# Second attention: the stores of its relative terms in halves of 64 rows, narrower by the columns that nothing reads

## The reference

```python
x = L0_attn_a_hidden_states
x = x + _L0_attn_a_ref(_layernorm(x, axis=-1),  ...)
x = x + _L0_ffn_ref(_layernorm(x, axis=-1),  ...)
x = x + _L0_attn_b_ref(_layernorm(x, axis=-1),  ...)
x = x + _L0_ffn_ref(_layernorm(x, axis=-1),  ...)
```

```python
def heads(x):
    return x.reshape(B, S, H, D).transpose(0, 2, 1, 3)
q = heads(hidden_states @ Wq + bq)
k = heads(hidden_states @ Wk + bk)
v = heads(hidden_states @ Wv + bv)
scores = jnp.einsum('bhqd,bhkd->bhqk', q, k)
pos_l = jnp.arange(S)[:, None]
pos_r = jnp.arange(S)[None, :]
dist_idx = pos_l - pos_r + M - 1
pos_emb = dist_emb[dist_idx]
rel_q = jnp.einsum('bhld,lrd->bhlr', q, pos_emb)
rel_k = jnp.einsum('bhrd,lrd->bhlr', k, pos_emb)
scores = (scores + rel_q + rel_k) / jnp.sqrt(jnp.asarray(D, scores.dtype))
probs = jax.nn.softmax(scores, axis=-1)
ctx = jnp.einsum('bhqk,bhkd->bhqd', probs, v)
ctx = ctx.transpose(0, 2, 1, 3).reshape(B, S, E)
```

## Time and profile before

| | us |
|---|---|
| median of 3 runs (4907.82 to 4912.31) | 4911.35 |
| the profiled execution | 4912.15 |
| its span | 4910.4 |
| stage b1 | 2244 to 3058 |
| stage b2 | 3058 to about 3950 |

### The profile page before, as it was taken

The page is one execution under the profiler, slowest core; times in us unless marked ns, Lnnn a source line. Parts: engine busy times, 40 slices in busy tenths (PEclk is TensorE's granted clock), DMA queues, the critical chain, the costliest instruction groups (busy, mean ns, idle before and its releaser), DMA issues.

```text
span 4910.4 us, 102424 instructions
## 1 busy us (share of the span) xinstructions
PE 3915.1 (80%) x31924; PEld 2380.9 (48%) x31924; DVE 2889.9 (59%) x6305; ACT 2635.3 (54%) x6550; POOL 1689.6 (34%) x1383
## 2 busy tenths in 40 slices
PE   2999999999488888734666565999999945888886
PEld 1555555554255555522222222677777723555554
DVE  2555555555577777543444443566666665777775
ACT  1555555554367777523333333566666624777774
POOL 0000000000588888523222222111111116878774
PEclk9999999999799999965555555999999977999998
DMA  3222222221111111027999999777777711111111
GB/s 118 87 78 78 78 78 80 81 78 53 49 25 23 27 27 23 17 71 293 380 381 385 380 381 369 269 262 260 248 272 250 256 43 52 25 26 25 25 23 32
DMA packets 374686, 701.06 MB, mean 143 GB/s; under 512 B 54180, under 2 KB 161016, under 8 KB 374568
## 3 DMA queue, kind: packets, MB, share of 16 engines
q1 hardware_dynamic: 330536, 565.25, 33.6%
q0 software_dynamic: 44032, 134.30, 7.4%
HBM read 336.53 MB, written 314.64 MB: 133 GB/s over the span
## 4 chain that ended last, share of the span: by engine, by line
PE 51%; DMA 13%; DVE 10%; issue 9%; POOL 7%; ACT 4%; SPq 2%; DVEq 1%; POOLq 0%; ACTq 0%
DMA rel_k<-b_stage_k 12%; PE ps L332 5%; PE ps L1465 5%; PE ps L340 5%; PE ps L351 5%; PE ps L1474 5%; PE ps L1456 3%; PE ps L1485 3%; DVE f_rs L1028 2%; POOL f_rn L758 2%; PE ps L866 2%; DVE f_rc L1025 2%; POOL f_rot L756 2%; PE ps L1357 2%; DVE b_stage_k L1381 2%
## 5 line engine op out<-in xcount | busy, mean ns | idle before, releaser
L1381 DVE COPY b_stage_k<-ps 128x640 f32<-128x640 f32 (+2 forms) x512 | 359.1, 722 | 469.6 <-DMA rel_k<-b_stage_k 410.3
L430 ACT ACTIVATE a_p<-a_s,a_min 128x512 f32<-128x512 f32 x512 | 366.0, 715 | 470.3 <-DVE a_min L474 470.3
L1378 ACT ACTIVATE b_stage_q<-ps 128x640 f32<-128x640 f32 (+2 forms) x512 | 316.0, 624 | 505.4 <-PE ps L1360 388.0
L474 DVE CUSTOM_DVE_ANT_0 a_s<-ps,a_table 128x512 f32<-128x512 f32 x512 | 333.5, 689 | 374.5 <-PE ps L332 371.9
L1539 ACT ACTIVATE c_p<-c_s,c_min 128x512 f32<-128x512 f32 x512 | 370.2, 723 | 290.7 <-PE ps L1474 180.3
L1357 PE MATMUL ps<-b_e,b_st_k 48*128 48x512 bf16 (+1 forms) x512 | 305.9, 597 | 261.1 <-DVE b_stage_k L1381 261.1
L1574 DVE CUSTOM_DVE_ANT_0 c_s<-ps,c_rq 128x512 f32<-128x512 f32 x512 | 352.8, 689 | 200.8 <-PE ps L1465 188.1
L188 POOL COPY y<-ln_rows 128x512 f32 x32 | 19.9, 621 | 1304.8 <-DVE ln_rows L180 1304.8
L949 ACT ACTIVATE f_p<-f_s,f_min 128x128 f32<-128x128 f32 x1024 | 396.3, 390 | 89.1 <-DVE f_min L1014 88.7
L756 POOL TENSOR_TENSOR f_rot<-f_rc,f_rs 128x1024 f32<-128x1024 f32 x128 | 302.9, 2367 | 255.6 <-DVE f_rs L1028 255.3
L758 POOL TENSOR_TENSOR f_rn<-f_ss,f_power 128x16 f32<-128x16 f32 x128 | 373.8, 2920 | 14.9 <-DVE f_ss L1037 1.4
(11 more groups left out here) (171 smaller groups left out, 9194.5 us busy)
## 6 DMA issues: line engine op xcount, KB each, us to landing
rel_q<-b_stage_q SPq DMA_DIRECT2D x64, 1280.0 KB, 7.8
rel_k<-b_stage_k SPq DMA_DIRECT2D x64, 1280.0 KB, 7.7
c_rq<-rel_q SPq DMA_DIRECT2D x64, 1024.0 KB, 7.7
c_rk<-rel_k POOLq DMA_DIRECT2D x64, 1024.0 KB, 11.9
a_table<-skew_bias SPq DMA_DIRECT2D x64, 896.0 KB, 4.6
f_vb<-f_v SPq DMA_DIRECT2D x256, 128.0 KB, 2.4
rel_k<-b_stage_k SPq DMA_DIRECT2D x32, 1024.0 KB, 9.5
rel_q<-b_stage_q SPq DMA_DIRECT2D x32, 1024.0 KB, 5.3
```

What stands on the lines that cost most here:

```text
L430: nc.scalar.activation(a_p[:, lt % 2, h, :], a_s[:, lt % 2, h, :], ACT.Exp, bias=a_min[:, lt % 2, h:h + 1], scale=-1.0, accum_out=a_sum[:, ...
L1381: moves_b1(dve, 1, lambda out, src: nc.vector.tensor_copy(out, src))
```

## The change

1. span() leaves out columns that the shifted reads never touch, and starts or ends at odd columns. For q the widths of the four row tiles become 512, 639, 511 and 383 (before 640, 640, 512, 384), for k 384, 512, 639 and 511 (before 384, 512, 640, 640).
2. The strip lies in PSUM from column 0 of its bank, and the second matmul remains only where the strip is wider than 512: row tile 1 for q and 2 for k.
3. Each store is split in two, one of the upper and one of the lower 64 rows of the row tile, each 64 columns narrower than the span: row p is only read from column 127 - p on, over 512 columns at most.
4. For row tile 0 of q and row tile 3 of k, 127 columns are no longer stored. What stood there repeats columns 255 further on (q) or back (k), and reads() gives the second attention's transfers as pairs: one from the strip as before, one of 128 columns from those copies. c_rq and c_rk get five transfers per unit instead of four.

The counts of the semaphores follow. The diff:

```diff
--- before.py
+++ after.py
@@ -1298,12 +1298,20 @@
     b_st_stored = [starting("b_st_stored0", 32), starting("b_st_stored1", 32)]
     b_rel_full = [starting("b_relq_full", 32), starting("b_relk_full", 32)]
     b_rel_moved = [starting("b_relq_moved", 2), starting("b_relk_moved", 2)]
-    b_rel_stored = [[starting("b_relq_stored0", 16), starting("b_relq_stored1", 16)],
-                    [starting("b_relk_stored0", 16), starting("b_relk_stored1", 16)]]
+    b_rel_stored = [[starting("b_relq_stored0", 32), starting("b_relq_stored1", 32)],
+                    [starting("b_relk_stored0", 32), starting("b_relk_stored1", 32)]]
 
     def span(n, t):
 
-        return (P * max(0, t - 1), WIN) if n == 0 else (0, min(WIN, P * (t + 3)))
+        if n == 0:
+            return (P - 1 if t == 0 else P * (t - 1), WIN - 1)
+        return (0, WIN - 1 - P if t == LT - 1 else min(WIN - 1, P * (t + 3)))
+
+    def reads(n, t):
+
+        if n == 0:
+            return [(0, P, DIST_B), (P, SEQ, 0)] if t == 0 else [(P * (t - 1), SEQ, 0)]
+        return [(0, SEQ - P, 0), (SEQ - P, SEQ, -DIST_B)] if t == LT - 1 else [(0, min(SEQ, P * (t + 2)), 0)]
 
     def unit_loop(eng, step):
         with eng.Fori(0, UNITS_B // 2) as i:
@@ -1333,15 +1341,17 @@
                 for n in range(2):
                     lo, hi = span(n, lt)
                     hold(sp, b_rel_moved[n], u * 16 + (lt * QB + QB + 2))
-                    dst = bass.AP(rel_dram[n].tensor,
-                                  (u // QB) * (LT * HB * P * WIN) + (u % QB) * (QB * P * WIN) + (lt * HB * P * WIN + lo),
-                                  [[WIN, P], [P * WIN, QB], [1, hi - lo]])
-                    sp.dma_start(dst, b_stage[n][:, lt % 2, :, lo:hi]).then_inc(b_rel_stored[n][lt % 2], 16)
+                    for g in range(2):
+                        f, t = (lo + P // 2, hi) if g == 0 else (lo, hi - P // 2)
+                        dst = bass.AP(rel_dram[n].tensor, (u // QB) * (LT * HB * P * WIN) + (u % QB) * (QB * P * WIN)
+                                      + (lt * HB * P * WIN + g * (P // 2) * WIN + f), [[WIN, P // 2], [P * WIN, QB], [1, t - f]])
+                        sp.dma_start(dst, b_stage[n][g * (P // 2):(g + 1) * (P // 2), lt % 2, :, f:t]
+                                     ).then_inc(b_rel_stored[n][lt % 2], 16)
         unit_loop(sp, step)
         for n in range(2):
             sp.wait_ge(b_st_stored[n], 32 + 32 * (UNITS_B // 2))
             for q in range(2):
-                sp.wait_ge(b_rel_stored[n][q], 16 + 16 * (UNITS_B * 2))
+                sp.wait_ge(b_rel_stored[n][q], 32 + 32 * (UNITS_B * 2))
 
     def tensor_b1(pe):
         def step(u, q, i):
@@ -1354,10 +1364,10 @@
                         pe.wait_ge(b_rel_moved[n], u * 16 + (lt * QB + h + 1))
                         w = b_st[n][:, q, h, lt * P:(lt + 1) * P]
                         lo, hi = span(n, lt)
-                        last = nc.tensor.matmul(ps[:, bank, lo:min(hi, 512)], w, b_e[:, n, at + lo:at + min(hi, 512)],
-                                                start=True, stop=True)
-                        if hi > 512:
-                            last = nc.tensor.matmul(ps[:, bank + 1, 0:hi - 512], w, b_e[:, n, at + 512:at + hi],
+                        mid = min(hi, lo + SEQ)
+                        last = nc.tensor.matmul(ps[:, bank, 0:mid - lo], w, b_e[:, n, at + lo:at + mid], start=True, stop=True)
+                        if hi > mid:
+                            last = nc.tensor.matmul(ps[:, bank + 1, 0:hi - mid], w, b_e[:, n, at + mid:at + hi],
                                                     start=True, stop=True)
                         last.then_inc(b_rel_full[n], 1)
         unit_loop(pe, step)
@@ -1365,12 +1375,12 @@
     def moves_b1(eng, n, move):
         def step(u, q, i):
             for lt in range(LT):
-                eng.wait_ge(b_rel_stored[n][lt % 2], u * 32 + (16 * (lt // 2) + 16))
+                eng.wait_ge(b_rel_stored[n][lt % 2], u * 64 + (32 * (lt // 2) + 32))
                 for h in range(QB):
                     bank = 4 * n + 2 * (h % 2)
                     eng.wait_ge(b_rel_full[n], u * 16 + (lt * QB + h + 33))
                     lo, hi = span(n, lt)
-                    move(b_stage[n][:, lt % 2, h, lo:hi], ps[:, bank:bank + 2, :].rearrange("p b n -> p (b n)")[:, lo:hi])\
+                    move(b_stage[n][:, lt % 2, h, lo:hi], ps[:, bank:bank + 2, :].rearrange("p b n -> p (b n)")[:, 0:hi - lo])\
                         .then_inc(b_rel_moved[n], 1)
         unit_loop(eng, step)
 
@@ -1425,9 +1435,10 @@
             pool.dma_start(c_st[:, q, :, :, :].rearrange("p n h t -> p n (h t)"),
                            stack_dram[u].rearrange("n p h t -> p n (h t)")).then_inc(c_loaded[q], 16)
             for rt in range(LT):
-                src = bass.AP(rel_dram[1].tensor, (u // QB) * (LT * HB * P * WIN) + (u % QB) * (QB * P * WIN)
-                              + (rt * HB * P * WIN + P - 1), [[WIN - 1, P], [P * WIN, QB], [1, min(SEQ, P * (rt + 2))]])
-                pool.dma_start(c_rk[:, q, rt, :, 0:min(SEQ, P * (rt + 2))], src).then_inc(c_loaded[q], 16)
+                for f, t, by in reads(1, rt):
+                    src = bass.AP(rel_dram[1].tensor, (u // QB) * (LT * HB * P * WIN) + (u % QB) * (QB * P * WIN)
+                                  + (rt * HB * P * WIN + P - 1 + f + by), [[WIN - 1, P], [P * WIN, QB], [1, t - f]])
+                    pool.dma_start(c_rk[:, q, rt, :, f:t], src).then_inc(c_loaded[q], 16)
             hold(pool, c_pv, u * LT + 4)
             for h in range(QB):
                 nc.gpsimd.tensor_copy(c_v[:, q, :, h, 0:DB],
@@ -1438,11 +1449,11 @@
     def sync_b2(sp):
         def step(u, q, i):
             for lt in range(LT):
-                lo = P * max(0, lt - 1)
                 hold(sp, c_biased, u * TILES + (QB * lt + 12))
-                src = bass.AP(rel_dram[0].tensor, (u // QB) * (LT * HB * P * WIN) + (u % QB) * (QB * P * WIN)
-                              + (lt * HB * P * WIN + P - 1 + lo), [[WIN - 1, P], [P * WIN, QB], [1, SEQ - lo]])
-                sp.dma_start(c_rq[:, lt, :, lo:SEQ], src).then_inc(c_rq_loaded[lt], 16)
+                for f, t, by in reads(0, lt):
+                    src = bass.AP(rel_dram[0].tensor, (u // QB) * (LT * HB * P * WIN) + (u % QB) * (QB * P * WIN)
+                                  + (lt * HB * P * WIN + P - 1 + f + by), [[WIN - 1, P], [P * WIN, QB], [1, t - f]])
+                    sp.dma_start(c_rq[:, lt, :, f:t], src).then_inc(c_rq_loaded[lt], 16)
         unit_loop(sp, step)
 
     def tensor_b2(pe):
@@ -1451,7 +1462,7 @@
         def scores(u, q, a):
             lt, h, r = a // QB, a % QB, SCORE_BANKS[a % 4]
             if a == 0:
-                pe.wait_ge(c_loaded[q], (u // 2) * 80 + 80)
+                pe.wait_ge(c_loaded[q], (u // 2) * 96 + 96)
             pe.wait_ge(c_biased, u * TILES + (a + 21))
             nc.tensor.matmul(ps[:, r, :], c_st[:, q, 0, h, lt * P:(lt + 1) * P], c_st[:, q, 1, h, :],
                              start=True, stop=False)
@@ -1567,7 +1578,7 @@
         def bias_and_min(u, q, a):
             lt, h, r = a // QB, a % QB, a % 2
             if h == 0:
-                dve.wait_ge(c_rq_loaded[lt], u * 16 + 16)
+                dve.wait_ge(c_rq_loaded[lt], (u + 1) * (16 * len(reads(0, lt))))
             dve.wait_ge(c_scored, u * TILES + (a + 33))
             dve.wait_ge(c_exped, u * TILES + (a + 1))
             dve.sem_inc(gate, 1)
```

## The result

| | median, us | runs |
|---|---|---|
| before | 4910.84 | 4 (4907.82 to 4912.31) |
| changed | 5044.57 | 4 (5036.45 to 5048.31) |

The changed kernel takes 1.0271 times the time of the kernel before, with a 95% interval of 1.0253 to 1.0289: it is 134 us slower. The prediction had the direction and the stage, and twice the size (+276 us, 5187).

A forecast was written before the change was run, and what follows sets the result against it. The prediction took DMA to bound the stage that stores the relative terms; 4912.15 us plus 275 for slower 64-row stores plus 1 for reading gave 5188, predicted as 5187 us, range 4975 to 5395.

The forecast's parts named there:

- What bounds the stage: Stage writing the relative terms: bound by DMA alone, 9.70 MB per unit at 382 GB/s, 25.4 us.
- The rate of a store of 64 rows: Store stage: 64-row stores run at 230 GB/s, 33.8 us per unit instead of 25.2, +275 us.
- The two short stretches of the earlier trace: Feed-forward value copies in two 64-row halves, 233 GB/s at full share; 48-row stack stores at the stage's start, 230 GB/s.
- the paragraph on mixing: Store stage: halves follow each other unless some engines run a half ahead; half mixed gives 27.4 us per unit, +70 us.
- The DMA share: Store stage after the change: share still near 1.0, GB/s near 245; well below 1 would mean waiting for issue or SyncE.
- SyncE's issues: Store stage: sixteen stores per unit instead of eight, 0.37 us each, +3.0 us per unit, hidden in 13.9 us of waiting.
- Copies, matmuls: Store stage: fewer second matmuls and narrower copies; both engines wait for DMA, gain below 1 us at the stage's end.
- Unaligned rows: Stores beginning at columns 191, 127 or 319: nothing to 8%, at most 82 us; taken as nothing.
- The reading stage: Second attention's reads: same bytes, two of eight transfers cut in two, hidden except at the start; taken as +1 us.
- Rival A: Store stage: the halves overlap and the saved bytes arrive, 4781 us; decided above a mean 315 GB/s; chance 0.12.
- Rival B: Store stage: the halves are mixed half of the time, about 4982 us, 4900 to 5070; chance 0.10.
- outer range: Whole kernel: 4975 to 5395 us, taking in the forecast, two thirds of B and most of C, leaving out A.

The follow-up runs named there:

- the parity run: Kernel before with each store split into its even and its odd rows, full width: 4911.80 us, 0.9996 of the time before.
- the run with two queues: Changed kernel with stores of rows 64 to 127 issued from ScalarE's queue, SyncE storing only rows 0 to 63: 4969.73 us, 1.0109 of the time before.
- the split by heads: Kernel before with each store split into two of 128 rows and two heads each: 4913.74 us, 0.9996 of the time before.
- the run with the columns alone: Changed kernel with narrower spans and paired reads, but one store of 128 rows per row tile: 4878.57 us, 0.9931 of the time before.
- the runs on order: Changed kernel with upper rows of q and k stored before lower rows: 5164.59 us; with each 64-row store cut again by heads, halves alternating: 5090.20 us.

## Why the prediction was right in kind and twice too large

*What bounds the stage.* Right: the stage is bound by DMA, the bytes over the rate give the unit (8.12 MB at 276 GB/s is 29.4 us, as the stage's length over 32 says), and the loss lies in it: 127.5 of 135.7 us.

*The rate of a store of 64 rows.* This is the term that was mis-sized. It took 230 GB/s for the stores alone, 33.8 us per unit; measured were 276 GB/s for everything that moves, 29.4 us. Without the 1.9 us for stack stores and loads the stores themselves take 27.5 us, which is 267 GB/s. The two short stretches of the earlier trace rows had the mechanism right and its size wrong: they last a microsecond each, one reads 48 rows, and the other is a copy within SBUF that reads 64 rows and writes 64 others. A saturated stream of halves behaves otherwise, and how much so depends on order (263 to 308 over the share). The step that failed is the sentence "I take 230 GB/s": a rate from a microsecond was put in for a stream, though the paragraph on mixing named what would relieve it. Half mixed, worked out there as +70 us, and no mixing, +275, lie on either side of the 134 measured; by the same formula 27.5 us would be a third mixed, an estimate that puts the lower DMA share down to mixing too. Why the short stretches carried so little stays open: stores that were made to begin together still carried 272 over the share.

*The DMA share.* Wrong: 0.92 and not near 1. Two queues raise the share to 0.96, more and smaller stores lower it to 0.86, which fits a part of SyncE's single queue in it. That some engines have nothing queued, because one that is held up keeps the queue full for the others, is argued, not shown; no view here shows single DMA engines. The prediction had named a share well below 1 as the sign that stores wait for issue and not for rows. That sign misled: the rows decide all the same, as the parity run shows (share 1.02 with as many stores) and the run with two queues (SyncE waiting, the loss still there).

*SyncE's issues.* The number of issues is hidden, as forecast (the split by heads costs nothing). But the term was too small, since a store of 64 rows takes at least 0.60 us to issue and not 0.37. And the forecast counted on SyncE's 13.9 us of waiting per unit as cover, and those are gone in the changed kernel, taken up by issues that last longer.

*Copies, matmuls.* As forecast of no weight; PE's busy share in the stage is 0.51, for the 0.45 that belonged to a longer unit.

*Unaligned rows.* Taken at nothing, and nearly so: the run with the columns alone keeps 374 GB/s, 2% less than before. The reading of the starts was wrong in part: only row tile 0 of q begins at odd columns (191 and 127), 319 is a width, and the other stores begin at multiples of 64.

*The reading stage.* Nothing in the middle, as forecast (the fifth c_rk of a unit is issued in GpSimd's idle time, and PE stays busy throughout). At the start +0.1 us, from the last store's landing to the first matmul, where +1 was taken.

*Rival A,* that the halves overlap and the bytes arrive, needed 315 GB/s for the stores. Rival B, half mixed, came nearest: its range of 4900 to 5070 holds the measured time, which lies below the forecast's own 5070 to 5350, and the runs on order speak for its mechanism. That the outer range of 4975 to 5395 holds it too is owed to this rival, with its chance of 0.10, and not to the forecast's sum.

## What to carry to other kernels

Where a stage is bound by DMA, a store of rows 0 to 63 or 64 to 127 of SBUF costs more than half of a store of all 128: split by heads or by parity of rows, which cost nothing here, and save bytes only with shapes whose rows are spread over all 128. If a cut into halves can't be avoided, let the halves alternate store by store; both longer stretches on one half and smaller stores were slower here. A rate that is read from a microsecond tells the mechanism and not the size; one run of the stream is worth more than both short stretches.

## What the runs showed of the hardware

- Rows 0 to 63 and 64 to 127 in a store each: 289 GB/s in the stage; even and odd rows in a store each: 382. Only the place of the rows differs, in SBUF and in DRAM.
- The order of the same 64-row stores changes the time by 120 us: 245 GB/s when two stores of one half follow each other, 276 when halves alternate.
- Where SyncE has waited before it, a store of 128 rows takes 0.37 us to issue and one of 64 neighbouring rows 0.60. In the dense stream of the changed kernel it mostly takes 1 to 2 us, and so it does in the parity run, which loses nothing. In the chain of waits this looks like a bound on SyncE.
- 64-row stores from two queues: 298 GB/s, with SyncE waiting for 294 of 700 us; from one queue 276.
- Odd columns, in one start of eight and five widths of eight, cost at most 2% of the rate (374 GB/s instead of 382).
